# The last group of an expert stage: which engine makes the gated products, in what order the gates, their transfers and their transposes go

## The reference

```python
x = _L0_conv_ref(x, ...)                 # softmax attention over 4096 tokens, 4 images, 128 channels
t = _to_tokens(x)                        # (4, 4096, 128)
t = t + _L1_attn_ref(_ln_t(t), W_kv, q_proj)      # 8 heads, running max and running sums along the tokens
t = t + _L1_ffn_ref(_ln_t(t), router_w, router_b, expert_w, expert_b)
x = _from_tokens(t, x)
# _L1_ffn_ref(x):
router_probs = softmax(x @ router_w + router_b)          # 8 experts
top_p, top_i = top_k(router_probs, 2); top_p = top_p / sum(top_p)
expert_out = einsum('bnd,edc->bnec', x, expert_w) + expert_b
out = einsum('bnk,bnkc->bnc', top_p, take(expert_out, top_i))
```

## Time and profile before

| | before |
|---|---|
| median of three runs | 2675.07 us |
| the profiled execution | 2673.73 us, its span 2672.0 us |
| TensorE busy in the span | 2531.1 us (95%) |
| VectorE | 2196.7 us (82%) |
| GpSimd | 2048.4 us (77%) |
| ScalarE | 1852.4 us (69%) |

### The profile page before, as it was taken

One profiled execution on the slowest core, in us unless ns is written; L12 is line 12 of the kernel. 1 busy time (PEld: TensorE's weight loads), 2 busy tenths in 40 slices (PEclk: granted clock), 3 DMA queues, 4 the chain that ended last, 5 costly groups with the idle time before them and its releaser, 6 DMA issues.

```text
span 2672.0 us, 36315 instructions
## 1 busy us (share of the span) xinstructions
PE 2531.1 (95%) x10665; PEld 1840.1 (69%) x10665; DVE 2196.7 (82%) x3277; ACT 1852.4 (69%) x3406; POOL 2048.4 (77%) x1505
## 2 busy tenths in 40 slices
PE   6999999999999999999999999998879999999877
PEld 4888877788887788888778788875445555555433
DVE  6788887788888788888778888872789898998994
ACT  5677777667777777767776667776887777777640
POOL 4787877778886778877688777885458989888884
PEclk9999999999999999999999999999999999999989
DMA  1000000010000010000000100101436576565645
GB/s 67 5 13 9 9 13 9 13 40 9 12 13 9 9 40 9 13 13 9 9 9 13 36 9 9 44 21 52 175 121 235 200 257 229 196 233 201 238 183 186
DMA packets 58102, 198.35 MB, mean 74 GB/s; under 512 B 12752, under 2 KB 15376, under 8 KB 40496
## 3 DMA queue, kind: packets, MB, share of 16 engines
q1 hardware_dynamic: 57904, 196.03, 20.8%
HBM read 178.04 MB, written 17.96 MB: 73 GB/s over the span
## 4 chain that ended last, share of the span: by engine, by line
PE 48%; POOL 25%; issue 14%; DVE 7%; ACT 4%; DMA 1%; POOLq 0%; SPq 0%; DVEq 0%; ACTq 0%
POOL p_lo L220 22%; PE m_ps L358 5%; PE om_ps L387 5%; PE s_ps L373 5%; PE om_ps L389 5%; PE om_ps L388 5%; PE s_ps L374 5%; PE s_ps L375 5%; PE mo_ps L1244 4%; PE k_ps L1200 1%; DVE v_ps L1429 1%; PE row_ps L1224 1%; DVE ay L1437 1%; PE v_ps L1200 1%; PE k_ps L1202 1%
## 5 line engine op out<-in xcount | busy, mean ns | idle before, releaser
L220 POOL TENSOR_TENSOR p_lo<-pf,p_hi 128x512 fp32r<-128x512 f32 x1024 | 1319.5, 1293 | 390.5 <-ACT p_hi L510 387.9
L505 ACT ACTIVATE pf<-s_ps 128x512 f32<-128x512 f32 x1024 | 613.2, 599 | 508.4 <-PE s_ps L375 506.9
L649 DVE TENSOR_REDUCE mx<-m_ps 128x1 f32<-128x512 f32 x1024 | 701.7, 686 | 255.4 <-PE m_ps L358 248.3
L665 DVE TENSOR_TENSOR sum_ps<-sum_ps,pf 128x512 f32<-128x512 f32 x960 | 662.1, 690 | 19.9 <-ACT pf L505 19.5
L510 ACT CAST p_hi<-pf 128x512 fp32r<-128x512 f32 x1024 | 627.3, 613 | 0.0
L373 PE MATMUL s_ps<-q_hi,kd_hi 128*128 128x512 f32 x1024 | 425.2, 415 | 0.0
L358 PE MATMUL m_ps<-w_both,q_hi 128*128 128x512 f32 x1024 | 405.8, 397 | 7.2 <-DVE mx L649 6.0
L387 PE MATMUL om_ps<-p_hi,v_hi 128*128 128x512 f32 x1024 | 402.4, 393 | 6.0 <-POOL p_lo L220 6.0
L374 PE MATMUL s_ps<-q_hi,kd_lo 128*128 128x512 f32 x1024 | 400.3, 391 | 0.0
L375 PE MATMUL s_ps<-q_lo,kd_hi 128*128 128x512 f32 x1024 | 400.3, 391 | 0.0
L388 PE MATMUL om_ps<-p_hi,v_lo 128*128 128x512 f32 x1024 | 399.6, 390 | 0.0
(11 more groups left out here) (221 smaller groups left out, 3600.1 us busy)
## 6 DMA issues: line engine op xcount, KB each, us to landing
bq<-weight_rows SPq DMA_DIRECT2D x64, 1024.0 KB, 6.7
gate_b<-gate_rows SPq DMA_DIRECT2D x64, 1024.0 KB, 4.8
xb<-in_x_dram SPq DMA_DIRECT2D x8, 1024.0 KB, 6.1
rb_sb<-inverse_rows SPq DMA_DIRECT2D x32, 256.0 KB, 4.0
tokens<-xb SPq DMA_DIRECT2D x32, 256.0 KB, 2.0
tp<-tokens SPq DMA_DIRECT2D x32, 256.0 KB, 5.2
rb<-norm_rows SPq DMA_DIRECT2D x32, 256.0 KB, 5.4
tv<-tokens SPq DMA_DIRECT2D x32, 256.0 KB, 5.9
```

Source lines behind the costliest of these rows:

```text
L220: nc.gpsimd.tensor_tensor(p_lo[:, r, :], pf[:, r, :], p_hi[:, r, :].bitcast(F32), ALU.subtract).then_inc(lo_done, 1)
L505: nc.scalar.activation(pf[:, g % RING, :], s_ps[:, g % 2, :], ACT.Exp, scale=SCALE).then_inc(exp_done, 1)
L649: nc.vector.tensor_reduce(mx[:, n % 2, sub, chunk:chunk + 1], m_ps[:, j % 2, :], AX.X, ALU.max).then_inc(m_max, 1)
L665: nc.vector.tensor_tensor(sum_ps[:], sum_ps[:], p, ALU.add).then_inc(sum_done, 1)
```

## The change

The last group's work (`LAST`, block 28 on) is put in another order and on other engines:

- All products of blocks 28 to 31 are made on VectorE. Of the blocks before, VectorE makes the odd pairs of 25 and 27; block 26 is wholly GpSimd's.
- The gates of blocks 29 and 31 are spread into `bq`, the tile of the scan's weights, which is free by then. Spreads go out two blocks ahead, and those of blocks 28 and 29 directly behind the row transfers and ahead of the store of block 26. A spread waits for its own image's row transfer (`gr_out` is now four semaphores), not for all four.
- The last group's gates are drawn together: the end of `gates` comes in slot 3 rather than 4, ahead of `output` of block 26. ScalarE loads the table before the squares.
- For every group ScalarE makes 0.5 tanh + 0.5, as a second operation (`half` is a new constant). The differences before the two clamps (`v_r`, `var2`) go to PSUM instead of SBUF, and for the last group an added maximum puts the second largest logit in PSUM for `gap`.
- TensorE turns the last group's gates in slot 7 rather than 6, GpSimd waits for the last residual before it goes on, and one semaphore counts all stores.

```diff
-    FREE = NBLK - (F_LAG - V_LAG) - 1
+    FREE, LAST = NBLK - (F_LAG - V_LAG) - 1, NBLK - B
 ...
         def by_vector(f, p):
-            return f >= FREE and p % 2 == 1
+            return f >= LAST or (f >= FREE and f % 2 == 1 and p % 2 == 1)
 ...
+        def in_rows(f):
+            return f > LAST and (f - LAST) % 2 == 1
 ...
         def gate_pair(f, p):
-            return gb[:, p // 2, 2 * (p % 2):2 * (p % 2) + 2, :]
+            rows = bq if in_rows(f) else gb
+            return rows[:, p // 2, 2 * (p % 2):2 * (p % 2) + 2, :]
+
+        def spread_done(f, half):
+            if in_rows(f):
+                return gq_in[half], 16 * ((f - LAST) // 2 + 1)
+            return gb_in[half], 16 * (f + 1 - max(f - LAST, 0) // 2)
+
+        def share_slot(s):
+            return 3 if s == SUPERS - 1 else 4
 ...
             def gate_spread(i, j):
                 s, b, cols = place(i)
-                sp.wait_ge(gr_out, 16 * B * (s + 1))
-                if i:
-                    sp.wait_ge(xg_pool, pool_gated(i - 1, 2 * j + 1))
-                    after(sp, xg_dve, vector_gated(i - 1, 2 * j + 1))
+                sp.wait_ge(gr_out[b], 16 * (s + 1))
+                if i == LAST + 1:
+                    sp.wait_ge(z_dve, NBLK * HEADS)
+                    sp.wait_ge(a_act, NBLK * HEADS)
+                elif i:
+                    last = i - 2 if i > LAST else i - 1
+                    sp.wait_ge(xg_pool, pool_gated(last, 2 * j + 1))
+                    after(sp, xg_dve, vector_gated(last, 2 * j + 1))
 ...
-                if stage(f):
+                if stage(f) and f < LAST:
                     gate_spread(f, 1)
 ...
+                if f + 1 == LAST:
+                    gate_rows(SUPERS - 1)
+                    for i, half in ((LAST, 0), (LAST, 1), (LAST + 1, 0), (LAST + 1, 1)):
+                        gate_spread(i, half)
                 if stage(f - 1):
                     store(f - 1)
-                if stage(f + 1):
+                if stage(f + 1) and f + 1 < LAST:
 ...
+                if f in (LAST, LAST + 1):
+                    for half in range(2):
+                        gate_spread(f + 2, half)
 ...
                         add_halves(v - 1)
+                        if v == NBLK:
+                            pool.wait_ge(t2_dve, NBLK)
 ...
-                    if norm2_at(j, 2) is not None and h == 6:
+                    if norm2_at(j, 2) is not None and h == (7 if norm2_at(j, 2) == SUPERS - 1 else 6):
                         turn_gates(norm2_at(j, 2))
 ...
+                    if norm2_at(j, 1) == SUPERS - 1 and h == 0:
+                        nc.scalar.preload_act_table_set("natural_log_exp_and_others")
 ...
                         nc.scalar.activation(share[:], gap[:], ACT.Tanh, scale=0.5).then_inc(th_act, 1)
+                        act.wait_ge(th_act, s + 1)
+                        nc.scalar.activation(share[:], share[:], ACT.Identity, bias=half[:], scale=0.5).then_inc(share_act, 1)
 ...
-                nc.vector.tensor_tensor(v_r[:], st_ps[:], v_r[:], ALU.subtract).then_inc(diff_dve, 1)
+                nc.vector.tensor_tensor(st_ps[:], st_ps[:], v_r[:], ALU.subtract).then_inc(diff_dve, 1)
                 dve.wait_ge(diff_dve, s)
-                nc.vector.tensor_scalar(v_r[:], v_r[:], 0.0, None, ALU.max).then_inc(var_dve, 1)
+                nc.vector.tensor_scalar(v_r[:], st_ps[:], 0.0, None, ALU.max).then_inc(var_dve, 1)
 ...
-                nc.vector.tensor_scalar(var2[:], var2[:], 0.0, None, ALU.max).then_inc(var2_dve, 1)
+                nc.vector.tensor_scalar(var2[:].unsqueeze(2), x[:, :, 3 * E:3 * E + 1], 0.0, None, ALU.max).then_inc(var2_dve, 1)
 ...
-                    nc.vector.tensor_tensor(gap[:], top1[:], top2[:], ALU.subtract).then_inc(gate, 1)
+                    second = top2[:].unsqueeze(2)
+                    if s == SUPERS - 1:
+                        second = x[:, :, 3 * E:3 * E + 1]
+                        nc.vector.tensor_reduce(second.rearrange("p g o -> p (g o)"), lg, AX.X, ALU.max).then_inc(top_ps, 1)
+                        dve.wait_ge(top_ps, 1)
+                    nc.vector.tensor_tensor(gap[:].unsqueeze(2), top1[:].unsqueeze(2), second, ALU.subtract).then_inc(gate, 1)
 ...
-                if slot == 4:
+                if slot == share_slot(s):
                     dve.wait_ge(clr, 1)
-                    dve.wait_ge(th_act, s + 1)
-                    nc.vector.tensor_scalar(share[:], share[:], 0.5, 0.5, ALU.mult, ALU.add).then_inc(gate, 1)
+                    dve.wait_ge(share_act, s + 1)
```

More of the change, by code:

```diff
@@ L832, in scan_attention_and_experts @@
     PAIRS = E // 2
-    GATE = 22
+    GATE = 21
     FAR = 1.0e30
@@ L860, in scan_attention_and_experts @@
         zeros = sb("zeros", [C, TOK])
-        epsc, ones = sb("epsc1", [C, 1]), sb("ones", [C, 1])
+        epsc, ones, half = sb("epsc1", [C, 1]), sb("ones", [C, 1]), sb("half", [C, 1])
         xf = sb("xf", [C, TOK])
@@ L891, in scan_attention_and_experts @@
         tv_in = [sem(f"tv_in{i}") for i in range(NV)]
-        t_out = [sem(f"t_out{i}") for i in range(NV)]
+        t_out = sem("t_out")
         b_in = [sem(f"b_in{i}") for i in range(3)]
@@ L942, in by_vector @@
         def by_vector(f, p):
-            return f >= FREE and p % 2 == 1
+            return f >= LAST or (f >= FREE and f % 2 == 1 and p % 2 == 1)
         def vector_gated(f, p):
-            return max(f - FREE, 0) * (PAIRS // 2) + ((p + 1) // 2 if f >= FREE else 0)
+            return sum(by_vector(g, q) for g in range(FREE, f + 1) for q in range(PAIRS) if (g, q) <= (f, p))
         def pool_gated(f, p):
             return f * PAIRS + p + 1 - vector_gated(f, p)
+        def in_rows(f):
+            return f > LAST and (f - LAST) % 2 == 1
         def pair_at(j, h):
@@ L1127, in run_gpsimd @@
             nc.gpsimd.memset(ones[:], 1.0).then_inc(cst1, 1)
-            pool.wait_ge(cst1, 3)
+            nc.gpsimd.memset(half[:], 0.5).then_inc(cst1, 1)
+            pool.wait_ge(cst1, 4)
             for e in range(E):
@@ L1322, in hold_logits @@
                 act.wait_ge(lg_pe, s + 1)
-                after(act, gr_out, 16 * B * s)
+                for b in range(B):
+                    after(act, gr_out[b], 16 * s)
                 nc.scalar.copy(l_sb[:], st_ps[:]).then_inc(lg_act, 1)
```

47 lines of the change are left out of this document (25 added, 22 removed).

## The result

| | before | after |
|---|---|---|
| median of five runs | 2675.07 us (2673.47 to 2676.49) | 2660.07 us (2658.96 to 2660.51) |
| span of the profiled execution | 2672.0 us | 2658.3 us |

The ratio is 0.9941, 95% interval 0.9931 to 0.9952: the change makes the kernel 15.0 us faster. The forecast was 11.5 us and its range ended at 2660.4, so the direction was right and the size was not: the time lies 0.3 us under the range.

The account below looks back on a forecast made before the run. After the scan no engine is full, so the last 74 us were taken as a chain of waits. Tail -10.2 and scan -1.3 us gave -11.5, so 2675.07 us becomes 2663.6, range 2660.4 to 2668.4.

Parts of the forecast that it names:

- Steps 1, 2 and 3: Block 31's residual to gates `g32`: unblocked residual -2.14 us, covered table load -0.88, shorter way from last pick to `g32` -3.3.
- Step 5: Last group's transposes on TensorE: they wait for GpSimd's block 26 products, not the gates, and come 3.0 us earlier.
- Steps 6 and 7: Transposes to block 28's first product, 10.61 to 8.45 us; then four last blocks to the end, 35.4 to 30.4.
- Rival B: Last group's spreads: the burst of four lands late, TensorE waits 1 to 3 us, +2, 2665.6 us; chance 0.12.
- step 6: Transposes to block 28's first product at TensorE: earlier spread and VectorE's faster product, -2.16 us.
- the tail: From block 31's residual to TensorE's end: -3.0 - 2.2 - 5.0 = -10.2 us.
- step 7: Blocks 28 to 31 with products on VectorE alone: TensorE is the bound, 30.4 us instead of 35.4, -5.0.
- Rival D: Tail: TensorE's clock falls as its waits lie differently; at the lower level throughout +30 us, 2694; chance 0.02.
- The scan: Scan phase: 0.2 us from the `var2` clamp and 1.1 from `share`, together -1.3 us, bounds +1 and -4.
- rival C: Scan phase: the removed stalls were on the path after all, up to 4 us instead of 1.3, 2661; chance 0.11.
- `share`: Scan gates: halving moved to ScalarE takes about 0.18 us off TensorE's wait, six times, -1.1 us.

Follow-up runs that it names:

- t4: Changed kernel with the last group's table load back in its old place behind the squares; 2661.11 us, ratio 0.9939 to the kernel before.
- t7: Changed kernel with `gap` again made from two SBUF tiles, without the maximum into PSUM; 2657.97 us, ratio 0.9937 to the kernel before.
- t2: Changed kernel with the last group's transposes back in slot 6; 2658.21 us, ratio 0.9929 to the kernel before.
- t1: Changed kernel without GpSimd's wait for the last residual; 2662.51 us, ratio 0.9946 to the kernel before.
- v2: Changed kernel with six throwaway matmuls filling TensorE's wait ahead of block 28; 2661.39 us, ratio 0.9939 to the kernel before.
- u1: Changed kernel with its three scan edits taken back, leaving the last group's edits; 2661.95 us, ratio 0.9941 to the kernel before.
- v1: Kernel before with twelve throwaway matmuls filling TensorE's wait ahead of block 28; 2673.83 us against 2677.40, ratio 0.9989.
- t3: Changed kernel with the even pairs of blocks 28 to 31 back on GpSimd; 2669.66 us, ratio 0.9970 to the kernel before.
- u2: Changed kernel run again unchanged, on the same chip as the kernel before; 2659.78 us, ratio 0.9931.

## Why the prediction missed its size

**Steps 1, 2 and 3, the gates, -6.3 us: right but for 0.8.** Residual 0.69 (0.67 forecast), logarithm right behind the clamp, `g32` 13.57 us after the residual's start, where steps 1 to 3 made it 19.09 - 6.3 = 12.8. The difference is the 1.30 of L1545, of which some 0.3 were counted (ScalarE's two steps lie beside it). I had taken it that any PSUM operand frees the operation; here one with its output alone in PSUM stood. The Trainium skill puts it so (GPSIMD Engine Reference, "8. Key points": contention with VectorE instructions "with two SBUF inputs"), and the trace agrees: L1545 has two such inputs and took 1.30 us.

**Step 5, GpSimd is late next, -3.0: right.** The transposes came 15.91 us after the residual instead of 19.14, -3.2; TensorE waited 0.33 us for GpSimd's fourth product of block 26 and for no gate; t4 and t7, with gates 0.2 and 0.4 us later, left the transposes in place to 0.1; and t2 gave the 0.86 of the slot to 0.01.

**Steps 6 and 7, the steps that failed.** What they forecast for the changed kernel lies within 1.3 us of its two traces: 8.45 us from the transposes to block 28 (measured 9.33 with a landing of 5.31, and 8.23 with one of 4.22) and 30.4 from there to the end (30.83 and 29.15). The bias costs 0.46 a block rather than 0.86 (7.34 less 16 x 0.43). Rival B, the late second half, made VectorE wait 1.30 in one trace and 0.47 in the other, and TensorE's block 28 was longer by 0.12 for it in the second; in t1, t7 and v2, with waits of 0.9 to 1.1, by 0.4 to 0.6. What failed is the other side of the difference, the cost of before that steps 6 and 7 subtract from: 10.61 and 35.4 are from the one trace of six in which the spread landed within 4.4 us, GpSimd's product came first and TensorE's clock didn't fall. In the other five they are 12.3 to 12.5 and 37.2 to 38.4. So the change gives -3.1 to -4.2 in step 6 and -6.4 to -9.2 in step 7, and the tail -13 to -16 (69.35 less 56.07 and less 53.30) rather than -10.2; by time, u1 has -16.5 for the edits of the tail alone. The changed kernel has no second engine at that spread to lose to and waits 1.1 to 2.2 us instead of 4.2; its clock fell there more seldom, and in v1's trace it stayed up behind a shorter wait.

**Rival D had the right mechanism and the wrong side.** I asked whether the change makes the clock fall, found 1.00 in 2640 to 2650, and gave it 0.02. It falls at block 28, with the old last group in five traces of six, and the change makes it rarer (with the last products all on VectorE two of twelve traces, the first and t4's; and in t3, behind a wait of 4.36).

**The scan, -1.3: right in kind, short in size; rival C is out.** By the medians of u1 and u2 it is -2.2, by undisturbed traces -2.0, within the bound of -4. That the 13 us of stall of the clamps give almost nothing held. `share` was the term that I mis-sized, -1.1 for -2.0: I gave it 0.18 a group, but in the first group it was itself stalled, for 0.5 us, and I had not read its row. That makes 1.6; the other 0.4 I can't place. In before, over the span:

```profile
L1510 DVE TENSOR_SCALAR share<-share x8: 148/150/673, 1996.7 to 2620.7; 128x16 f32<-128x16 f32 x8
```

The -4.39 of the first pair is thus 0.2 from before block 0, 2.0 of the edits, about 0.8 of a clock dip, and the rest variation between blocks 22 and 31 (196.77 us in the first trace, 195.0 in the second of the same kernel), whose cause I leave open.

**The sum.** The two peculiarities of that one trace, a scan too long by 2.6 and a tail too short by 4.2, nearly cancel in its span (2672.0 against 2674.2), which is why the span gave no warning. But the scan's excess was in no term of mine and the tail's shortfall in two. The times held a sign of it: those of the kernel before spread from 2671.9 to 2682.3 us in all comparisons, those of the changed kernel from 2658.5 to 2660.9.

## What to carry to other kernels

A chain of waits read from one trace gives the time of that execution; before a step of it is subtracted, ask which of its rows hang on whether a transfer lands before or after another engine is free, or on a wait behind which the clock may fall, and give the other outcome a price as well, best from a second trace. Where two engines wait for the same transfer and hold each other up, the second waits for the first's operation to end, and giving all of that work to the faster one took 9.07 us a block to 7.34. A stall that is removed from one small operation reappears on the next one that reads two SBUF tiles while the other engine is still at work.

## What I had not expected of the hardware

- A VectorE operation with two SBUF inputs and a PSUM output stands still beside GpSimd as one with an SBUF output does: 1.30 us instead of 0.29 (L1545). The same shape with one input in PSUM took 0.29 to 0.30 in the rows beside it.
- With both engines waiting for one spread, VectorE began 0.04 to 0.05 us ahead wherever it was free (seven traces), and GpSimd's 128x1024 product took 3.38 instead of 2.34; where the spread landed 0.3 us before VectorE was through with another operation, GpSimd began 0.20 ahead and VectorE's product took 3.22 instead of 1.22.
- TensorE's clock went to 0.50 for 3 to 7 us behind single waits of 2.2 to 4.4 us, with the engine full before and after, but not in every execution: behind 2.24 it fell, behind 2.37 in another trace it didn't.
- The added ScalarE operation on 128x16 took 0.31 us with a bias tile and Identity, the tanh of the same size without one 0.22.
- With four 1 MB spreads sent within 3 us, the first landed 5.3 us after its issue in one trace and 4.2 in another; with two sent, in 4.4 us in one trace and in 4.9 to 5.2 in six.
